# Means and score rows of a two-layer graph kernel sent through memory, T's unit 7 moved, VectorE reordered

## What is computed

```python
h = relu(layernorm(x))
Xw = h @ Wv + bv
sj, si = Xw @ aw[:d, 0], Xw @ aw[d:, 0]
e = leaky_relu(sj[:, None, :] + si[:, :, None] + ab[0], 0.2)
alpha = adj * exp(e)
T = alpha / (sum(alpha, -1) + 1e-12)
H = (h @ Wk[0] + bk[0]) + (T @ h @ Wk[1] + bk[1]) + (T @ T @ h @ Wk[2] + bk[2])
x = x + relu(H)                                   # layer 0
h = relu(layernorm(x))
Ah = adj + I;  dh = rsqrt(sum(Ah, -1))
out = x + relu(dh * (Ah @ (dh * h)) @ kernel + bias)   # layer 1
```

## Time and profile before

| | |
|---|---|
| time, median of 3 runs | 773.44 us (772.76 to 775.34) |
| time of the profiled execution | 773.69 us |
| its span | 771.9 us, 14180 instructions |
| granted TensorE clock, mean | 0.998 of full speed |
| TensorE busy | 759.4 us, 98% |
| VectorE busy | 610.0 us, 79% |
| ScalarE busy | 540.0 us, 70% |
| GpSimd busy | 188.5 us, 24% |

### The profile page before, as it was taken

How to read it: one execution, slowest core, us unless ns; L and a number is a source line. 1 busy time by engine, 2 the same in 40 slices (tenths; PEclk the granted TensorE clock), 3 DMA queues, 4 the chain that set the end, 5 groups by cost and what they waited for, 6 DMA issues and landing times.

```text
span 771.9 us, 14180 instructions
## 1 busy us (share of the span) xinstructions
PE 759.4 (98%) x5190; PEld 696.2 (90%) x5190; DVE 610.0 (79%) x1417; ACT 540.0 (70%) x1051; POOL 188.5 (24%) x190
## 2 busy tenths in 40 slices
PE   8799999999999999999999999999999999999997
PEld 8598988989899898998989989899998989889986
DVE  7897788678896789967889678886888777895665
ACT  3898797667965779657885578955698567976351
POOL 3031240312403123130321305122050322402330
PEclk9999999999999999999999999999999999999999
DMA  7566339714497055960568505784248733456411
GB/s 228 207 229 208 111 134 326 234 73 137 156 320 251 11 169 175 301 229 3 176 218 304 175 20 186 252 277 140 74 148 299 246 108 113 136 203 211 137 64 54
DMA packets 60661, 135.93 MB, mean 176 GB/s; under 512 B 6320, under 2 KB 32304, under 8 KB 60592
## 3 DMA queue, kind: packets, MB, share of 16 engines
q1 hardware_dynamic: 51824, 104.35, 41.0%
q10 hardware_dynamic: 8768, 30.68, 11.4%
HBM read 126.62 MB, written 8.39 MB: 175 GB/s over the span
## 4 chain that ended last, share of the span: by engine, by line
PE 91%; ACT 4%; DVE 3%; issue 1%; POOL 0%; POOLq 0%; ACTq 0%
PE acc L1139 16%; PE acc L1141 16%; PE acc L1140 16%; PE da L999 11%; PE db L999 6%; PE da L1107 4%; PE da L1109 4%; PE da L1108 4%; PE tp L1107 4%; PE tp L1109 4%; PE tp L1108 4%; ACT tg_e L483 1%; PE acc L1037 1%; PE acc L1030 1%; ACT g_hi L451 1%
## 5 line engine op out<-in xcount | busy, mean ns | idle before, releaser
L1139 PE MATMUL acc<-g_hi,t_hi 128*128 128x256 f32 (+1 forms) x1024 | 291.9, 285 | 2.8 <-DVE g_lo L735 2.8
L1141 PE MATMUL acc<-g_hi,t_lo 128*128 128x256 f32 (+1 forms) x1024 | 290.2, 283 | 0.0
L1140 PE MATMUL acc<-g_lo,t_hi 128*128 128x256 f32 x1024 | 289.4, 283 | 0.0
L1139 PEld LDWEIGHTS acc<-g_hi,t_hi 128*128 128x128 f32 x1024 | 194.0, 189 | 3.8 <-issue 3.2
L1140 PEld LDWEIGHTS acc<-g_lo,t_hi 128*128 128x128 f32 x1024 | 194.6, 190 | 0.3
L1141 PEld LDWEIGHTS acc<-g_hi,t_lo 128*128 128x128 f32 x1024 | 194.5, 190 | 0.0
L368 POOL TENSOR_TENSOR g_lo<-tmp,g_hi 128x256 fp32r<-128x256 f32 x64 | 59.7, 933 | 265.0 <-ACT g_hi L536 265.0
L483 ACT ACTIVATE tg_e<-si,sij 128x256 f32<-128x256 f32 x256 | 109.2, 500 | 4.0 <-DVE sij L722 3.9
L772 DVE TENSOR_TENSOR a_lo<-a_raw,a_hi 128x512 fp32r<-128x512 f32 x128 | 89.6, 720 | 25.2 <-ACT a_hi L526 25.1
L363 POOL TENSOR_TENSOR rstd<-ve,mhalf 128x2 f32<-128x2 f32 (+2 forms) x41 | 50.4, 1229 | 184.3 <-DVE ve L672 145.0
L536 ACT CAST g_hi<-tmp 128x256 fp32r<-128x256 f32 x64 | 25.9, 405 | 98.4 <-DVE tmp L786 98.4
(11 more groups left out here) (146 smaller groups left out, 1598.7 us busy)
## 6 DMA issues: line engine op xcount, KB each, us to landing
a_raw<-adj_dram SPq DMA_DIRECT2D x64, 512.0 KB, 4.7
a_raw<-adj_z_dram SPq DMA_DIRECT2D x64, 512.0 KB, 4.0
tg_a<-adj_t_dram ACTq DMA_DIRECT2D x58, 512.0 KB, 4.4
x_o<-x_dram SPq DMA_DIRECT2D x64, 128.0 KB, 3.1
...
tg_a<-adj_t_dram SPq DMA_DIRECT2D x6, 512.0 KB, 4.6
```

The costliest lines, as they stand in the source:

```text
L1139: nc.tensor.matmul(acc[:, s, 0:n], l_hi, r_hi, start=(jt == 0), stop=False)
L1140: nc.tensor.matmul(acc[:, s, 0:D], l_hi, r_lo, start=False, stop=False)
L1141: ins = nc.tensor.matmul(acc[:, s, 0:n], l_lo, r_hi, start=False, stop=(jt == NT - 1))
```

## The change

**Rows through memory.** The means are transposed once, as 128 x 8 columns to 8 rows of 128, and the scores twice, as 128 x 4 to 4 rows of 128. ScalarE copies each result to a small tile in SBUF, SyncE writes it to a tensor in device memory, waits for the write, and reads it back broadcast to 128 partitions into `si`. The mean rows use `si` too, between the last use of the old scores and the new ones. `si_rows`, `layer0_end` and the old `si_copy` are gone: 16 transposes per boundary between two batches become 3, at 7 boundaries.

**T's unit 7** gets its `leaky` and `exponent` behind g1_hi of chunk 0 of the next U (until now only for batch 0), its product on VectorE behind chunk 1, its high part behind chunk 2, its low part behind chunk 3. Unit 4's product moves from V to Z. In the dense stage `leaky` and `exponent` of unit 0 move from tiles 4 and 5 to tile 7.

**VectorE** makes p0 and `sij` of a tile ahead of g2_lo, takes the second `centre` of the stage behind tile 2 and not ahead of it, and makes the statistics of the next x behind chunks 0 and 1 of U and not 0 to 3. Two of the row sums of ScalarE move from U to the dense stage.

```diff
-    STATS_U = {0: (0, 1), 1: (2, 3), 2: (4, 5), 3: (6, 7)}
+    STATS_U = {0: (0, 1, 2, 3), 1: (4, 5, 6, 7)}
...
+            def mean_over_partitions(b):
+                sp.wait_ge(mean_t_ready, b)
+                sp.dma_start(mean_dram, mean_t).then_inc(mean_stored, 16)
+                sp.wait_ge(mean_stored, 16 * b)
+                sp.wait_ge(leaky_done, b * NU)
+                sp.dma_start(si[:, :], mean_dram.rearrange("t (o p) -> o (t p)", o=1).to_broadcast([P, N])).then_inc(mean_loaded, 16)
+            def si_over_partitions(b, h):
+                sp.wait_ge(si_t_ready, 2 * (b - 1) + h + 1)
+                sp.dma_start(si_dram[h], si_t).then_inc(si_stored, 16)
+                sp.wait_ge(si_stored, 16 * (2 * (b - 1) + h + 1))
+                sp.wait_ge(xt_centred, (b - 1) * NG + 2 * h + 2)
+                sp.dma_start(si[:, h * HJ * P:(h + 1) * HJ * P],
+                             si_dram[h].rearrange("(o t) p -> o (t p)", o=1).to_broadcast([P, HJ * P])).then_inc(si_loaded[h], 16)
...
+                    if i == 1 and left > 0 and b > 0:
+                        mean_over_partitions(b + 1)
...
+                    if i == 2 and left > 0:
+                        si_over_partitions(b + 1, 0)
+                        si_over_partitions(b + 1, 1)
...
+            def mean_copy(b):
+                act.wait_ge(mean_full, b)
+                nc.scalar.copy(mean_t, mean_bank).then_inc(mean_t_ready, 1)
...
-            def si_copy(b, g):
-                act.wait_ge(si_full, b * NG + g + 1)
-                nc.scalar.copy(si[:, g * 2 * P:(g + 1) * 2 * P],
-                               acc[:, SI_SLOT, g % 2 * 2 * P:(g % 2 + 1) * 2 * P]).then_inc(si_ready, 1)
+            def si_copy(b, h):
+                act.wait_ge(si_t_full, 2 * (b - 1) + h + 1)
+                if h == 1:
+                    act.wait_ge(si_stored, 16 * (2 * b - 1))
+                nc.scalar.copy(si_t, si_bank).then_inc(si_t_ready, 1)
...
-                if u % 2 == 0:
-                    act.wait_ge(si_ready, b * NG + u // 2 + 1)
+                if b == 0 and u % 2 == 0:
+                    act.wait_ge(si_ready, u // 2 + 1)
+                elif b > 0 and u % HJ == 0:
+                    act.wait_ge(si_loaded[u // HJ], 16 * b)
...
             def centre(g, b):
                 dve.wait_ge(xt_loaded[g], 16 * b)
-                dve.wait_ge(mean_full, 2 * (b - 1) + g // 2 + 1)
-                row = mean_rows[g // 2][:, g % 2 * 2 * P:(g % 2 + 1) * 2 * P]
+                dve.wait_ge(mean_loaded, 16 * b)
+                row = si[:, g * 2 * P:(g + 1) * 2 * P]
...
-                for t in range(NT):
-                    ins = nc.tensor.transpose(mean_rows[t // HJ][:, t % HJ * P:(t % HJ + 1) * P],
-                                              mv0[:, t, 0:1].to_broadcast([P, P]), ident[:, :])
-                    if t % HJ == HJ - 1:
-                        ins.then_inc(mean_full, 1)
+                nc.tensor.transpose(mean_bank, mv0[:, :, 0], ident[:, :]).then_inc(mean_full, 1)
+            def si_turned(b, h):
+                if h == 0:
+                    pe.wait_ge(g1_tmp_ready, b * NT)
+                else:
+                    pe.wait_ge(si_t_ready, 2 * b - 1)
+                pe.wait_ge(p0_ready, b * NT + HJ * (h + 1))
+                nc.tensor.transpose(si_bank, sij[:, h * HJ:(h + 1) * HJ, 1], ident[:, :]).then_inc(si_t_full, 1)
...
-                               lambda jt: (g2_hi[:, jt, :], g2_lo[:, jt, :]))
+                               lambda jt: (g2_hi[:, jt, :], g2_lo[:, jt, :]),
+                               middle=(lambda: rows_of_mean(b + 1)) if i == (2 if b == 0 else 3) and not last else None)
...
                     if i == 2 and not last:
-                        pe.wait_ge(si_ready, (b + 2) * NG)
+                        pe.wait_ge(si_t_ready, 2 * (b + 1))
```

More of the change, by code:

```diff
@@ L154, in gnn_two_layers @@
         zt = [da, tp.rearrange("p g k c -> p g (k c)")]
-        mean_rows = [tp[:, r].rearrange("p k c -> p (k c)") for r in range(2)]
+        mean_bank = tp[0:NT, 0, 0, 0:P]
+        si_dram = nc.dram_tensor("si_rows_dram", (2, HJ, P), F32, kind="Internal").ap()
+        mean_dram = nc.dram_tensor("mean_rows_dram", (NT, P), F32, kind="Internal").ap()
         ht_first = [g1.rearrange("p t d -> p (t d)").rearrange("p (g k c) -> p g k c", g=NG, k=KD) for g1 in (g1_hi, g1_lo)]
@@ L379, in batch @@
                     g1_split(b, i)
-                    if i == (3 if b > 0 else -1) and not last:
+                    if i == (1 if b > 0 else -1) and not last:
                         power(rstd0, ve0, ve0_ready, b + 1, rstd0_ready)
@@ L506, in layer0_dense @@
                     dense0(b, t)
-                    if t % 2 == 0 and t > 0:
-                        si_copy(b, t // 2 - 1)
+                    if t == HJ:
+                        si_copy(b, 0)
                     after(t)
@@ L531, in batch @@
                         zt_high(b - 1, 1)
+                    if i == (2 if b == 0 else 3) and not last:
+                        mean_copy(b + 1)
                     if i >= NT - 2 and not last:
@@ L551, in after @@
                         a_round(b, 0, 1)
-                    if t == 4 and not last:
-                        leaky(b + 1, 0)
-                    if t == 5 and not last:
-                        exponent(b + 1, 0)
                     if t == 6:
@@ L559, in after @@
                         a_round(b, 1, 1)
+                        if not last:
+                            leaky(b + 1, 0)
+                            exponent(b + 1, 0)
                 if not last:
@@ L843, in batch @@
                     u_chunk(b, i)
+                    if not last and b > 0:
+                        for t in STATS_U.get(i, ()):
+                            stats0_of(b + 1, t)
+                        if i == 1:
+                            moments0(b + 1)
                     if i in (NT - 3, NT - 2) and not last:
@@ L852, in batch @@
                         t_low(b, low[i])
-                    if not last and b > 0:
-                        for t in STATS_U.get(i, ()):
-                            stats0_of(b + 1, t)
-                        if i == 3:
-                            moments0(b + 1)
                 def after(t):
-                    if t == (5 if b == 0 else 0):
+                    if t == 5:
                         dve.wait_ge(rows_done, b * NT + NT)
@@ L869, in after @@
                         diag(b, 1)
-                    if t == 6 and not last:
-                        t_prod(b + 1, 0)
                     if t == 7:
@@ L874, in after @@
                         a_low(b, 1, 1)
+                        if not last:
+                            t_prod(b + 1, 0)
                 if not last:
@@ L1123, in out_product, with accumulate @@
                                                     for f in range(KD)]).then_inc(out_full, 1)
-            def accumulate(b, phase, i, read, before, ready, n, rhs):
+            def accumulate(b, phase, i, read, before, ready, n, rhs, middle=None):
                 s = acc_slot(phase, i)
@@ L1134, in accumulate @@
                 for jt in range(NT):
+                    if jt == HJ and middle is not None:
+                        middle()
                     if ready is not None and i == 0:
@@ L1160, in batch @@
                 for i in range(NT):
-                    if i == 1 and not last:
-                        layer0_end(b + 1)
                     if i == 2 and not last:
-                        pe.wait_ge(si_ready, (b + 2) * NG)
+                        pe.wait_ge(si_t_ready, 2 * (b + 1))
                     accumulate(b, V_PHASE, i, v_tmp_done, g1_tmp_ready, g1_ready, D,
-                               lambda jt: (g1_hi[:, jt, :], g1_lo[:, jt, :]))
+                               lambda jt: (g1_hi[:, jt, :], g1_lo[:, jt, :]),
+                               middle=(lambda: si_turned(b + 1, 1)) if i == 0 and not last else None)
                 dense = b + 1 if last else b + 2
```

60 lines of the change are left out of this document (27 added, 33 removed).

## The result

The kernel after takes 767.59 us (median of 4 runs, 767.28 to 767.79), the kernel before 773.85 us (4 runs, 772.76 to 775.34): ratio 0.9913, 95% interval 0.9895 to 0.9932. It is 6.3 us faster; 12.1 us were forecast, and the end of the range, 767.0, is missed by 0.6 us.

The account below looks back on a forecast made before the run. TensorE, busy 98% of the span, was taken as the bound. 773.69 - 9.9 (transposes) - 4.3 (dense waits) + 1.8 (batch 0's mean rows) + 0.7 (layer 1) = 762.0, forecast as 761.7 us against the median; range 759.0 to 767.0.

Parts of the forecast that it names:

- the last term: Layer 1: helpers' delay overdraws the cover at zt_lo by 0.1 us per boundary, +0.7 us in all.
- both helpers enter layer 1 some 1 to 1.5 us later than now: After V: VectorE and ScalarE start layer 1 1 to 1.5 us late, while nothing reaches TensorE in V.
- they win some back: Layer 1: helpers recover time; ScalarE has one leaky and exponent less, VectorE one product more and one less; no size given.
- 0.47 us of cover: Layer 1: zt_lo ends at 680.78, TensorE's output product starts at 681.25, leaving 0.47 us before lateness costs.
- my first rival: Layer 1: the helpers' delay arrives in full, 0.5 to 1.0 us at 7 boundaries, 764.5 to 768 us; chance 0.18.
- one of the signs of being wrong that I gave: Layer 1: idle time ahead of output products or hs pieces would show that the helpers are late.
- The score rows: Dense stage's end and V: score rows through memory arrive at D + 18.8, delaying helpers but not TensorE in V.
- it waits 1.1 us: Dense stage's end: ScalarE, ready for leaky 0 at D + 17.7, waits 1.1 us for the score rows.
- The transposes and the dense stage: All 7 boundaries: 91 fewer transposes at 0.109 us save 9.9 us; vanished dense-stage waits save 4.3 us.
- The rival that keeps the waits in the dense stage: Dense stage: VectorE's pieces behind tiles 2 and 4 replace g2_lo, waits stay, 766.0 us; chance 0.08.
- the 272 ns transpose: TensorE's stream: a transpose costs its listed 272 ns, so 24.8 us go in place of 9.9, 746.8 us; chance 0.04.
- The mean rows: Ahead of the dense stage: rows arrive in time with 0.9 us to spare, except in batch 0, +1.8 us once.

Follow-up runs that it names:

- run 5: Kernel after with unit 0's leaky and exponent at dense tiles 6 and 7 and product 1 back between V's chunks 0 and 1: 767.76 us.
- run 13: Kernel after with only unit 5's layer 1 steps put back (leaky, exponent, product one piece earlier; unit 4's high part one later): 763.71 us.
- run 10: Kernel after with unit 0 at dense tiles 6 and 7, product 1 behind V's chunk 0, unit 5's steps put back: 762.38 us.
- run 2: Kernel after with unit 4's product back behind chunk 7 of V: 770.41 us.
- run 6: Kernel before with VectorE's product 1 behind V's chunk 1 in place of chunk 0, nothing else: 780.6 us.
- run 7: Kernel after with only product 1 moved back between V's chunks 0 and 1: 769.85 us.
- run 9: Kernel after with unit 0 at dense tiles 6 and 7 and all old V and layer 1 numbers, unit 7 still in U: 766.77 us.
- run 11: Kernel after with all old V and layer 1 numbers, unit 0 left at the end of the dense stage: 769.68 us.
- run 4: Kernel after with VectorE's t_lo of unit 4 moved behind zt_lo: 764.33 us.
- run 12: Kernel after with old V and layer 1 numbers, unit 0 at tiles 6 and 7, batch 0's mean column copied two chunks earlier: 764.44 us.
- run 14: Kernel after with unit 0 at dense tiles 6 and 7 and unit 5's steps put back, product 1 left behind chunk 1: 766.13 us.
- run 16: Kernel after with unit 0, product 1, unit 5's steps put back, batch 0's mean column copied earlier, its leaky 0 left behind tile 7: 759.83 us.
- run 8: Kernel after with ScalarE's copy of batch 0's mean column at chunk 0 in place of 2: 765.23 us.

## Why the prediction was wrong

**The table of the layer 1 stages**, us behind layer 1's start on TensorE, tells it in short:

| kernel | V's chunk 7 | zt_lo | excess |
|---|---|---|---|
| before | 0.53 | 15.03 | 0.00 |
| after | 1.88 | 16.32 | 0.97 |
| V's beginning mended (run 5) | 1.22 | 16.21 | 0.86 |
| unit 5's steps mended (run 13) | 1.87 | 15.84 | 0.50 |
| both (run 10) | 1.23 | 15.20 | 0.00 |

The first two columns are of the last boundary, the excess of all middle batches. For the kernel after:

```profile
673.81 1.28 DVE L861 TENSOR_TENSOR zt_lo<-da,zt_hi 128x512 fp32r<-128x512 f32 x2
```

In every row with an excess it is the start of zt_lo less 15.35 us, and so it is in runs 2, 6, 7, 9 and 11 (zt_lo at 16.83, 16.19, 16.69, 15.74, 16.78). Exceptions are run 4, where the step ahead of zt_lo was moved behind it, and single batches of runs 12, 13, 14 and 16, which are 0.2 to 0.4 us longer than this gives. So zt_lo sets the stage, and each microsecond that it is late beyond 15.35 costs one, as the prediction has it.

**The step that failed** is the last term: "I expect this to be overdrawn by 0.1 us per boundary: +0.7 us". It measured +0.97 us at six boundaries and +1.2 at batch 0's, 7.0 us. The part before it was right in its size: "both helpers enter layer 1 some 1 to 1.5 us later than now"; VectorE's chunk 7 is 1.35 us later (1.15 where it stood at 0.73 before). Two things set against it were wrong.

- "they win some back": of the 1.35 us, 16.32 - 15.03 = 1.29 arrive at zt_lo. ScalarE's `leaky` 7 and VectorE's product 7, which left layer 1, stood behind zt_lo (`leaky` 7 at 685.36, 20.9 us behind layer 1's start), so they gave nothing at the tightest place; and unit 5's steps, which the change moves one piece later, take from it. With unit 5's steps in their old place (run 10) VectorE does win back: 0.70 us late at chunk 7, 0.17 at zt_lo.
- "0.47 us of cover": this was read from zt_lo's end to the product's start, in one boundary. By the 15.35 us above the cover was 0.32 us there, and 0.12 in the two batches where zt_lo started at 15.23.

1.29 less 0.32 is the 0.97. For the layer 1 stage I named only the steps of units 4 and 7 and gave unit 5's no row; product 1's new place in V I did not name at all. Runs 5, 13 and 10 show the split: with unit 5 mended the excess falls by 0.47, with V's beginning mended as well by the other 0.50, while V's beginning alone gives 0.11. The outcome was my first rival, at 0.18 ("0.5 to 1.0 us at 7 boundaries", 764.5 to 768), and one of the signs of being wrong that I gave, "ahead of the output products or hs pieces of layer 1". That rival had the size, not the two moved steps behind it.

**The score rows.** Copy, write, read and `leaky` 0 on their engines:

```profile
628.44 0.26 ACT L498 COPY bv_r<-acc 4x128 f32<-4x128 f32 x1
628.72 0.27 SPq L311 DMA_DIRECT2D si_rows_dram<-bv_r  x1
629.89 0.33 SPq L315 DMA_DIRECT2D si<-si_rows_dram  x1
...
635.32 1.71 ACT L523 ACTIVATE tg_e<-si,sij 128x256 f32<-128x256 f32 x4
```

"it waits 1.1 us" is wrong: the read is issued 1.17 us behind the write and takes 3.2 us (median of 14), 4.4 in place of 7.5, and `leaky` 0 waits for nothing; it is late because of its place in the order (at batch 0's boundary alone it waits, 0.16 us). It starts 17.7 us behind the dense start, where 18.8 was forecast. The hole on VectorE came all the same, but shorter and earlier: product 0 was to hold it from "about 20.1 to 22.8", and VectorE waits from 19.4 to 20.6 (1.15 us ahead of 638.15) and is done with the product at 21.8. What I missed is its partner, product 1 moved behind chunk 1; run 6 prices that alone at 7.3 us.

**The transposes and the dense stage** were right. Per boundary 2.15 us went, where 14.2 / 7 = 2.03 were forecast. A new transpose adds 0.12 us to the stream: 603.12 to 603.36 is 0.24, where one matmul is 0.12, so the 0.109 that I took for the 8-column form was fair and "nothing" was not. No wait is left in U, dense and V of the middle batches: each takes 65.86 us, the usual distances of its matmuls add up to 65.70, and no single distance is more than 0.09 us above the usual one. The rival that keeps the waits in the dense stage has not come, and neither has the 272 ns transpose. On the Trainium skill's 275 ns ("TensorE: Matmul & The Clock Gate", Part 4): the listed duration of the new transpose, 0.27 us, agrees with it; its cost in the stream, 0.12 us, doesn't.

**The mean rows** were right in both places. At the middle batches they are late by half a microsecond against the forecast: VectorE's `centre` waits 1.47 us for them and starts at 614.39 in the last boundary, 22.8 us behind U's start at 591.63, forecast 22.3. TensorE doesn't wait. In batch 0:

```profile
54.38 0.35 SPq L302 DMA_DIRECT2D mean_rows_dram<-bv_r  x1
...
56.59 0.35 SPq L306 DMA_DIRECT2D si<-mean_rows_dram  x1
...
62.00 0.69 DVE L741 TENSOR_TENSOR xt<-xt,si 128x512 f32<-128x512 f32 x1 [3.72 <-DMA si<-mean_rows_dram]
...
64.73 0.50 PE L1042 MATMUL da<-wa_hi,ht_hi 128*128 128x512 f32 x1 [1.73 <-DVE ht_lo L747]
```

Rows at 62.0 (forecast 61.8), 1.9 us lost on TensorE (forecast 1.8), and run 8 shows that the copy's place on ScalarE sets it.

**Left open.** Why unit 4's product is better in layer 1 than in V was not tried apart from runs 2 and 9. The two timelines say where the time lies, not why: between chunk 7 and zt_lo VectorE waits 1.60 us in run 9 (0.55, 0.72 and 0.33, all for ScalarE) and 1.14 in run 10 (0.59 for GpSimd, 0.55 for ScalarE). Product 1 and unit 5's steps put back with unit 0 left late was not run, so it isn't shown that unit 0's place is needed beside them. Batch 0's layer 1 still has 1.05 us of waits in run 16; they were not followed.
